# Splitting POOL's rounding of the next tile's inputs over two steps of a fused attention kernel

## The chip, the cores and the metric

One Trainium2 chip, one of its cores. The time is the device time of one execution of the program in microseconds (us); lower is better. PE is TensorE's matrix unit, DVE is VectorE, ACT is ScalarE, POOL is GpSimd, SP is the engine that issues most DMAs.

## The reference

The program is one block of a network on 1024 tokens (16 sequences of 64) of width 256: a gated cross-attention layer and a gated mixture of experts. Cut to what bears on the change:

```python
def _div_clamp_fp8(x, scale):
    y = jnp.clip(x.astype(jnp.float32) / scale, -FP8_MAX, FP8_MAX)
    y = y.astype(jnp.bfloat16).astype(jnp.float32)
    return _fp8_roundtrip(y)              # to float8_e4m3 and back

ln_out = _ln(hidden_states, ln_w, ln_b)
q  = _ln(_fp8_linear_pertensor(ln_out, wq,  ..., q_in_scale),  qln_w, qln_b)    # 16 heads of 128
k  = _ln(_fp8_linear_pertensor(ln_out, wk,  ..., k_in_scale),  kln_w, kln_b)    # 8 heads
v  = _fp8_linear_pertensor(ln_out, wv, ..., v_in_scale)
core = _gqa(q, k, v)                      # softmax attention, two q heads to a k head
qx = _ln(_fp8_linear_pertensor(ln_out, wqx, ..., qx_in_scale), qxln_w, qxln_b)
kx, vx = split(cond @ w_kv_x)             # from the context, kx normalised too
xout = _gqa(qx, kx, vx)
catq = _div_clamp_fp8(concatenate([core, xout]), proj_smooth)
x = x + tanh(g_xattn) * (catq @ wproj * scales)
x = x + tanh(g_ffn) * mixture_of_experts(layernorm(x))
```

Four times per token (for k, q, v and qx) the layer's input is divided by a vector of scales, clamped and rounded to the float8 grid before its projection.

## The kernel before

**Tiles and steps.** The tokens are 8 tiles of 128. Each tile takes four steps, c = 0 to 3, so the attention is 32 steps, numbered n = 4 t + c. `run_steps` (L95 on) writes the first and the last tile out and runs tiles 1 to 6 as a loop of the hardware. A step projects four banks of 512 columns (`BANKS`: k, q, q, v in steps 0 and 1, kx, qx, qx, vx in steps 2 and 3), turns the normalised heads of the step before (`head_transposes`), takes the scores of step n-2, the values of step n-3 and the output projection of step n-4. Each engine has its own hand-written order of the same steps, and semaphores alone tie them. After the attention come the router, the scatter of rows to expert slots, 22 expert units and the gather.

**TensorE in a step** (`step` under `block.tensor`): `project(t, c, 0)` (L868 for kx and vx, L876 for the others), `prob_transposes` (L911), `scores` (L903), `project` 1, `values` (L925), `output` (L935), `project` 2, `head_transposes` 0 (L894), `project` 3, `head_transposes` 1 and 2. `project` of k, q, v and qx waits on `xgrid_done`, t + 1: the rounded inputs of its tile lie in `xq`, a part of the buffer `arena`.

**ACT in a step**: it copies each projected bank out of PSUM (`evacuate`, L645; `values_out`, L653), copies the transposed probabilities (L690), scales bank 0 of the step before by its norm coefficients (`norm_bank0`, L666), takes the softmax's exponential (L685), copies the heads (`heads_out`, L680), and last takes the root of the step's variances (`roots`, L657 and L659), for which it waits for POOL's `va`.

**DVE in a step**: statistics of bank 0 (L1275), `softmax_in` (L1283, L1286), statistics of bank 1, `softmax_sum` (L1292, L1295, which gives `rinv`), statistics of bank 2 (its last one gives `bn_done`), `over_smooth` (L1302) and `quantise`, the five operations of `to_grid` on 1024 columns of 16-bit numbers (L1235, L1237, L1240, L1242, L1246). In step 1 it also does `inputs_magnitude` (L1251, L1253, L1256) for the next tile; in step 3 `residual` (L1316, L1319).

**POOL in a step**: `normalise` (L529, waits for `rinv`), `variance` (L503 and L505, waits for `bn_done`), `coefficients` (L511, L512, L513, L517: four short operations in a chain, of which the first waits for ACT's root), `norm_bank` 1 and 2 (L523). The inputs of tile t + 1 are made on the side, over the steps of tile t: the division in step 0 (`inputs_over_scale`, L472), the clamp and the magnitude by DVE in step 1, and the rounding at the end of step 2 (`inputs_round`, two operations: the addition of a big number, L495, and its subtraction, L497, which gives `xgrid_done`). Tile 0's inputs are made by DVE in the prologue, so POOL rounds seven times, for tiles 1 to 7. POOL's step lags TensorE's: while POOL is at the end of step 2, TensorE is in the later part of step 3.

Of the kernel before, what the change touches and what calls it, by code (L numbers as in the profile page):

```python
# [83 lines left out]
def ge(eng, sem, value):  # L84

    if isinstance(value, int) and value <= 0:
        return
    eng.wait_ge(sem, value)


def live(n, back):

    return not isinstance(n, int) or 0 <= n - back < 4 * NT
# [21 lines left out]
def build(nc, x, cols, rowc, ident, cen, tri, slot, ctxT, wkvN, wqN, wkN, wvN, wqxN, wpT, rwT, wffn, out):  # L115
    ctx = ExitStack()
    with ctx:
# [9 lines left out]
        NU = 4  # L127
# [331 lines left out]
        def _(gp):  # L459
# [4 lines left out]
            def load_output_weights():  # L464

                gp.wait_ge(ld_wkv, 16)
                gp.dma_start(wp[:, :, :], wpT.rearrange("(h p) o -> p h o", p=P)).then_inc(ld_wp, 16)

            def inputs_over_scale(T):
                gp.wait_ge(xT_evac, 4)  # L470
                ge(gp, xgrid_done, T)
                gp.tensor_tensor(xin[:, :].rearrange("p (j c t) -> p j c t", j=4, c=HC),  # L472
                                 xT[:, :, bass.ds(T * P, P)].unsqueeze(1).to_broadcast([P, 4, HC, P]),
                                 sinv[:, :].rearrange("p (j c) -> p j c", j=4).unsqueeze(3)
                                 .to_broadcast([P, 4, HC, P]), ALU.mult).then_inc(xin_done, 1)
# [9 lines left out]
            def chained(sem, ins, count):  # L485

                ins.then_inc(sem, 1)
                gp.wait_ge(sem, count)

            xin16 = xin[:, :].bitcast(F16)  # L490

            def inputs_round(T):

                gp.wait_ge(xmag_done, T + 1)
                gp.tensor_tensor(xin16, xin[:, :], xm[:, :], ALU.add).then_inc(xbig_done, 1)  # L495
                gp.wait_ge(xbig_done, T + 1)
                gp.tensor_tensor(xq[:, bass.ds(T * XW, XW)], xin16, xm[:, :], ALU.subtract).then_inc(xgrid_done, 1)  # L497

            def variance(n, x):

                gp.wait_ge(bn_done, n + 1)
                ge(gp, coef_done, n)
                gp.tensor_tensor(va[:, :], st[:, :, 2], epsc[:, x, :], ALU.add).then_inc(var_done, 1)  # L503
                gp.wait_ge(var_done, n + 1)
                gp.tensor_tensor(vw[:, :], va[:, :], newt[:, 0, :], ALU.mult).then_inc(achain, 1)  # L505

            def coefficients(n):

                gp.wait_ge(achain, n + 1)
                gp.wait_ge(root_done, n + 1)  # L510
                chained(nchain, gp.tensor_tensor(nw[:, 0, :], vw[:, :], r0[:, :], ALU.mult), 3 * n + 1)  # L511
                chained(nchain, gp.tensor_tensor(nw[:, 1, :], nw[:, 0, :], r0[:, :], ALU.mult), 3 * n + 2)  # L512
                chained(nchain, gp.tensor_tensor(nw[:, 0, :], nw[:, 1, :], newt[:, 1, :], ALU.add), 3 * n + 3)  # L513
                ge(gp, norm0_done, n)
                ge(gp, norm1_done, n)
                ge(gp, norm2_done, n)
                gp.tensor_tensor(cw[:, :], nw[:, 0, :], r0[:, :], ALU.mult).then_inc(coef_done, 1)  # L517

            def norm_bank(n, c, i):

                r = raw[c % 2][i].rearrange("p (h d) -> p h d", d=D)
                gp.wait_ge(coef_done, n + 1)
                gp.tensor_tensor(r, r, cw[:, 4 * i:4 * i + 4].unsqueeze(2).to_broadcast([P, 4, D]), ALU.mult)\  # L523
                  .then_inc((norm0_done, norm1_done, norm2_done)[i], 1)

            def normalise(w, s):
                gp.wait_ge(rinv_done, w + 1)
                ge(gp, probT_done, w - 1)
                gp.tensor_tensor(probn[s].rearrange("p (g t) -> p g t", t=S),  # L529
                                 prob[s].rearrange("p (g t) -> p g t", t=S),  # L530
                                 rinv[:, s, :].unsqueeze(2).to_broadcast([P, 8, S]),
                                 ALU.mult).then_inc(probn_done, 1)

            def step(t, c):
                n = NU * t + c
                proj, attend = live(n, 0), live(n, 2)
                if attend:
                    normalise(n - 2, c % 2)
                if proj:
                    variance(n, c // 2)  # L540
                    coefficients(n)
                    norm_bank(n, c, 1)
                    norm_bank(n, c, 2)
                if c == 0 and live(n, -NU):
                    inputs_over_scale(t + 1)
                if c == 2 and live(n, -NU):
                    inputs_round(t + 1)
                if isinstance(n, int) and n == 0:
                    load_output_weights()

# [15 lines left out]

            last = NU * NT
            run_steps(gp, step)
            normalise(last - 2, 0)
            twin_rows(0)  # L570
# [1036 lines left out]
```

## Time and profile before

| | us |
|---|---|
| median of 3 runs | 470.15 (469.44 to 470.99) |
| the profiled execution's own time | 468.51 |
| its span on the core | 466.7 |
| a tile of the loop (four steps) | 39.1 |
| busy share of PE, DVE, ACT, POOL over the span | 89, 80, 63, 60% |

A line of the trace gives the start in us, the duration, the engine, the line of the program, the operation, its output <- its inputs, partitions x elements, and how many operations of that kind stand in a row. In brackets behind it stands how long the engine had stood idle before it, and what ended that. Ends of matmuls are modelled: a line of PE can overlap the next one.

### The profile page before, as it was taken

The page shows a single profiled execution, that of the slowest core. Times are in us where ns is not written, and L with a number is a line of the kernel's source. Part 1 is how long each engine was busy: PE and PEld are TensorE (multiplying, and loading weights), DVE is VectorE, ACT ScalarE, POOL GpSimd, SP SyncE. Part 2 cuts the span into 40 slices and gives each one's busy share as a digit, 9 for nine tenths or more (in the row PEclk, how much of TensorE's full clock was granted, in tenths as well). Part 3 has the DMA queues.
Part 4 walks back from the last instruction along what each step waited for, and adds up shares of the span by engine and source line. Part 5 has one row for each costly group of instructions (what it writes and reads, how often), then busy time and mean ns, then how long its engine had stood idle before and what let it go on. Part 6 is the DMA issues. An engine that isn't in the chain of part 4 may idle for free.

```text
span 466.7 us, 10266 instructions
## 1 busy us (share of the span) xinstructions
PE 413.2 (89%) x3127; PEld 315.6 (68%) x3127; DVE 372.2 (80%) x837; ACT 295.5 (63%) x622; POOL 278.8 (60%) x401
## 2 busy tenths in 40 slices
PE   0488899999999999999999999999989496999980
PEld 0346667767776776777677677677679385999960
DVE  5887889999898999999989889999986763333247
ACT  3578967677776776767777677676882223566620
POOL 2055396686767759667676874965551571377650
PEclk9979999999999999999999999999997789999995
DMA  8944909999920000000000000000086122344308
GB/s 209 270 175 53 129 1 305 253 295 267 269 70 0 0 0 0 0 0 0 0 0 0 0 0 0 0 1 1 2 353 256 56 92 90 109 132 139 103 14 267
DMA packets 34812, 45.68 MB, mean 98 GB/s; under 512 B 3034, under 2 KB 32223, under 8 KB 33888
## 3 DMA queue, kind: packets, MB, share of 16 engines
q1 hardware_dynamic: 26656, 35.61, 25.7%
q0 software_dynamic: 6992, 9.46, 9.3%
q10 hardware_dynamic: 1136, 0.27, 0.3%
q8 instruction: 14, 0.23, 0.2%
q14 instruction: 14, 0.11, 0.1%
HBM read 28.34 MB, written 24.32 MB: 113 GB/s over the span
## 4 chain that ended last, share of the span: by engine, by line
PE 45%; DVE 17%; POOL 15%; issue 10%; ACT 7%; DMA 3%; ACTq 1%; POOLq 1%; SPq 0%; DVEq 0%
PE proj_ps L876 9%; PE score_ps L903 7%; PE pv_ps L925 4%; PE proj_ps L1036 4%; PE headT_ps L1036 4%; PE out_ps L935 4%; POOL xin L495 3%; POOL zbuf L564 3%; POOL rot L523 3%; DVE st L1275 3%; ACT rot L645 2%; PE headT_ps L894 2%; PE probT_ps L911 2%; POOL reg L529 2%; DVE yv L1302 2%
## 5 line engine op out<-in xcount | busy, mean ns | idle before, releaser
L876 PE MATMUL proj_ps<-arena 128*128 128x512 f16 x384 | 100.4, 385 | 3.9 <-POOL arena L497 3.9
L1275 DVE BATCH_NORM_STATS2 st<-rot 128x6 f32<-128x256 f32 x192 | 72.8, 421 | 14.2 <-ACT rot L645 13.2
L645 ACT ACTIVATE rot<-proj_ps 128x512 f32<-128x512 f32 x96 | 56.4, 587 | 20.7 <-PE proj_ps L876 19.1
L523 POOL TENSOR_TENSOR rot<-rot,cw 128x512 f32<-128x512 f32 x64 | 67.3, 1072 | 2.5
L529 POOL TENSOR_TENSOR reg<-reg,rinv 128x512 f32<-128x512 f32 x32 | 34.6, 1082 | 55.2 <-DVE rinv L1295 55.2
L903 PE MATMUL score_ps<-kT,qT 128*128 128x64 f32 x512 | 62.0, 275 | 0.6 <-ACT qT L680 0.5
L903 PEld LDWEIGHTS score_ps<-kT,qT 128*128 128x128 f32 x512 | 60.1, 193 | 2.4 <-ACT qT L680 2.2
L666 ACT ACTIVATE rot<-rot,cw 128x128 f32<-128x128 f32 x128 | 40.9, 390 | 30.3 <-POOL cw L517 30.3
L876 PEld LDWEIGHTS proj_ps<-arena 128*128 (+1 forms) x384 | 37.5, 103 | 29.8 <-issue 6.6
L868 PE MATMUL proj_ps<-arena 128*128 128x512 f16 x192 | 46.7, 379 | 0.0
L587 POOL DMA_INDIRECT ybuf<-arena,bslot x32 | 31.4, 983 | 19.1 <-issue 13.4
L925 PEld LDWEIGHTS pv_ps<-reg,vv 64*128 64x128 f32 x512 | 31.9, 192 | 14.5 <-issue 14.0
L1302 DVE TENSOR_TENSOR yv<-pv_ps,smi 128x512 bf16<-128x512 f32 x64 | 40.7, 677 | 0.0
L925 PE MATMUL pv_ps<-reg,vv 64*128 64x128 f32 x512 | 38.1, 290 | 1.9 <-DVE yv L1302 1.9
L935 PE MATMUL out_ps<-wp_sb,reg 128*128 128x256 bf16 x256 | 36.0, 287 | 4.2 <-DVE reg L1246 4.2
L894 PE MATMUL headT_ps<-idf,rot 128*128 128x128 f32 x256 | 38.5, 273 | 1.2 <-ACT kT L680 1.2
L511 POOL TENSOR_TENSOR nw<-vw,r 128x12 f32<-128x12 f32 x32 | 10.2, 320 | 42.5 <-ACT r L659 42.5
L894 PEld LDWEIGHTS headT_ps<-idf,rot 128*128 128x128 f32 x256 | 30.4, 141 | 7.4 <-issue 1.8
L685 ACT ACTIVATE reg<-reg 128x512 f32<-128x512 f32 x32 | 20.1, 628 | 23.9 <-DVE reg L1286 23.9
L935 PEld LDWEIGHTS out_ps<-wp_sb,reg 128*128 128x128 bf16 x256 | 23.5, 102 | 11.6 <-DVE reg L1246 4.9
L868 PEld LDWEIGHTS proj_ps<-arena 128*128 (+1 forms) x192 | 18.8, 98 | 15.5
L680 ACT ACTIVATE qT<-headT_ps,colv 128x512 f32<-128x512 f32 x32 | 24.9, 779 | 0.1
(220 smaller groups left out, 871.0 us busy)
## 6 DMA issues: line engine op xcount, KB each, us to landing
zbuf<-fill SPq DMA_DIRECT2D x1, 16576.5 KB, 64.4
arena<-in_wffn SPq DMA_DIRECT2D x4, 1536.0 KB, 13.6
arena<-zbuf SPq DMA_DIRECT2D x32, 128.5 KB, 2.1
wkv_stage<-in_wkvN SPq DMA_DIRECT2D x1, 2048.0 KB, 15.2
wp_sb<-in_wpT POOLq DMA_DIRECT2D x1, 2048.0 KB, 15.6
wp_sb<-ybuf SPq DMA_DIRECT2D x8, 256.0 KB, 4.6
xs<-in_x SPq DMA_DIRECT2D x2, 512.0 KB, 5.4
vv<-in_wqN POOLq DMA_DIRECT2D x1, 1024.0 KB, 12.6
```

Source lines behind the costliest of these rows:

```text
L523: gp.tensor_tensor(r, r, cw[:, 4 * i:4 * i + 4].unsqueeze(2).to_broadcast([P, 4, D]), ALU.mult)\
L529: gp.tensor_tensor(probn[s].rearrange("p (g t) -> p g t", t=S), prob[s].rearrange("p (g t) -> p g t", t=S), rinv[:, s, :].unsqueeze(2).to_ ...
L645: act.activation(raw[c % 2][i], proj_ps[i % 2][:, :], ACT.Copy).then_inc(proj_evac, 1)
L666: ins = act.activation(r, r, ACT.Copy, scale=cw[:, h:h + 1])
L868: mm = pe.matmul(ps, lhs, w[:, ch, o:o + 512], start=(k == 0), stop=(k == 5))
L876: mm = pe.matmul(ps, lhs, w[kind][:, ch, 512 * b:512 * b + 512], start=(k == 0), stop=(k == 3))
L894: mm = pe.transpose(dst, raw[c % 2][i][:, h * D:(h + 1) * D], idf[:, :])
L903: mm = pe.matmul(score_ps[:, (2 * g + b) * S:(2 * g + b + 1) * S], qT[:, s, 2 * g + b, :], kT[:, s, g, b * S:(b + 1) * S], start=True, sto ...
L925: mm = pe.matmul(pv_ps[b][:, g * P:(g + 1) * P], vv[rows, u, g * D:(g + 1) * D], pT[rows, g * P:(g + 1) * P], start=True, stop=True)
L935: mm = pe.matmul(out_ps[:, 0:H], catq[u % 2][:, h * P:(h + 1) * P], wp[:, 8 * u + h, :], start=(u == 0 and h == 0), stop=(u == NU - 1 and ...
L1275: ins = ve.bn_stats(st[:, 4 * i + h:4 * i + h + 2, :].rearrange("p h s -> p (h s)"), raw[c % 2][i][:, h * D:(h + 2) * D].rearrange("p (h d ...
L1302: ins = ve.tensor_tensor(y3[:, :, b * S:(b + 1) * S], pv_ps[b][:, :].rearrange("p (h t) -> p h t", t=S), smi[:, 8 * u:8 * u + 8].unsqueeze ...
```

## The change

`inputs_round` becomes two functions, and they are called at other places of POOL's order. The addition now stands in step 2 between `variance` and `coefficients`, the subtraction in step 3 between `variance` and `coefficients`. In both places ACT is about to take the root for which `coefficients` waits. Nothing is added or left out, no other engine's order is touched, and the semaphores are the same.

```diff
-            def inputs_round(T):
+            def inputs_big(T):
 
                 gp.wait_ge(xmag_done, T + 1)
                 gp.tensor_tensor(xin16, xin[:, :], xm[:, :], ALU.add).then_inc(xbig_done, 1)
+
+            def inputs_grid(T):
+
                 gp.wait_ge(xbig_done, T + 1)
                 gp.tensor_tensor(xq[:, bass.ds(T * XW, XW)], xin16, xm[:, :], ALU.subtract).then_inc(xgrid_done, 1)
...
                 if proj:
                     variance(n, c // 2)
+                if c == 2 and live(n, -NU):
+                    inputs_big(t + 1)
+                if c == 3 and live(n, -NU):
+                    inputs_grid(t + 1)
+                if proj:
                     coefficients(n)
                     norm_bank(n, c, 1)
                     norm_bank(n, c, 2)
                 if c == 0 and live(n, -NU):
                     inputs_over_scale(t + 1)
-                if c == 2 and live(n, -NU):
-                    inputs_round(t + 1)
```

POOL in the loop, from its `variance` of step 2 to its `coefficients` of step 3, before. REGISTER_ALU and ISA rows are address and semaphore work.

```order
L503 TENSOR_TENSOR va<-st,epsc 128x12
L505 TENSOR_TENSOR vw<-va,newt 128x12
L511 TENSOR_TENSOR nw<-vw,r 128x12
...
L517 TENSOR_TENSOR cw<-nw,r 128x12
L523 TENSOR_TENSOR rot<-rot,cw 128x512 x2
L494 REGISTER_ALU
L495 TENSOR_TENSOR xin<-xin,xm 128x1024
L497 ISA
L497 TENSOR_TENSOR arena<-xin,xm 128x1024
L529 TENSOR_TENSOR reg<-reg,rinv 128x512
...
L505 TENSOR_TENSOR vw<-va,newt 128x12
L511 TENSOR_TENSOR nw<-vw,r 128x12
```

The addition follows the two norm banks of step 2, and the subtraction follows the addition, ahead of step 3's `normalise`. Now the same stretch (the subtraction has become L500, L503 has become L506, and so on):

```order
L506 TENSOR_TENSOR va<-st,epsc 128x12
L508 TENSOR_TENSOR vw<-va,newt 128x12
L494 REGISTER_ALU
L495 TENSOR_TENSOR xin<-xin,xm 128x1024
L514 TENSOR_TENSOR nw<-vw,r 128x12
...
L526 TENSOR_TENSOR rot<-rot,cw 128x512 x2
L532 TENSOR_TENSOR reg<-reg,rinv 128x512
...
L508 TENSOR_TENSOR vw<-va,newt 128x12
L500 ISA
L500 TENSOR_TENSOR arena<-xin,xm 128x1024
L514 TENSOR_TENSOR nw<-vw,r 128x12
```

The addition has moved up past the four coefficient operations and the two norm banks. The subtraction has moved down past step 3's `normalise` and `variance`, so it now stands behind POOL's waits for `rinv` and for `bn_done` of step 3.

## Rows read from the trace of the kernel before

**Rows 1.** The page: busy time of each engine and its share of the span.

```profile
PE 413.2 (89%) x3127; PEld 315.6 (68%) x3127; DVE 372.2 (80%) x837; ACT 295.5 (63%) x622; POOL 278.8 (60%) x401
```

**Rows 2.** Busy time in one tile: stretch, length, each engine's busy us (operations), TensorE's granted clock.

```profile
144.01:183.14 39.13, 38.40 (x296) 27.97 (x297) 36.23 (x74) 27.80 (x61) 27.94 (x40) 1.00 0.00 0
```

**Rows 3.** The timeline of PE where one tile passes to the next.

```profile
178.95 1.03 PE L876 MATMUL proj_ps<-arena 128*128 128x512 f16 x4
...
180.25 1.46 PE L868 MATMUL proj_ps<-arena 128*128 128x512 f16 x6
...
181.98 0.60 PE L894 MATMUL headT_ps<-idf,rot 128*128 128x128 f32 x4
...
183.14 1.03 PE L876 MATMUL proj_ps<-arena 128*128 128x512 f16 x4 [0.56 <-POOL arena L497]
...
184.31 0.65 PE L911 MATMUL probT_ps<-idf,reg 128*128 128x128 f32 x4
```

**Rows 4.** The timeline of POOL from step 2's variance to step 3's normalise.

```profile
173.10 0.21 POOL L505 TENSOR_TENSOR vw<-va,newt 128x12 f32<-128x12 f32 x1
174.30 0.27 POOL L511 TENSOR_TENSOR nw<-vw,r 128x12 f32<-128x12 f32 x1 [0.99 <-ACT r L659]
...
175.84 0.65 POOL L517 TENSOR_TENSOR cw<-nw,r 128x12 f32<-128x12 f32 x1
...
178.56 2.13 POOL L495 TENSOR_TENSOR xin<-xin,xm 128x1024 f16<-128x1024 bf16 x1
180.88 2.12 POOL L497 TENSOR_TENSOR arena<-xin,xm 128x1024 f16 x1 [0.19 <-POOL xin L495]
182.96 1.22 POOL L529 TENSOR_TENSOR reg<-reg,rinv 128x512 f32<-128x512 f32 x1
```

**Rows 5.** The timeline of DVE in the same stretch.

```profile
173.61 0.43 DVE L1235 TENSOR_SCALAR yv<-yv 128x1024 bf16<-128x1024 bf16 x1
...
175.72 0.69 DVE L1246 TENSOR_TENSOR reg<-ys,ym 128x1024 bf16<-128x1024 f16 x1
...
179.82 0.20 DVE L1295 RECIPROCAL rinv<-sm 128x8 f32<-128x8 f32 x1
180.64 0.77 DVE L1275 BATCH_NORM_STATS2 st<-rot 128x6 f32<-128x256 f32 x2 [0.62 <-ACT rot L645]
...
182.63 0.65 DVE L1235 TENSOR_SCALAR yv<-yv 128x1024 bf16<-128x1024 bf16 x1
...
183.32 1.15 DVE L1237 TENSOR_SCALAR ya<-yv 128x1024 uint16<-128x1024 uint16 x1
```

**Rows 6.** The timeline of ACT in the same stretch.

```profile
176.52 1.28 ACT L666 ACTIVATE rot<-rot,cw 128x128 f32<-128x128 f32 x4 [1.34 <-POOL cw L517]
177.70 0.57 ACT L645 ACTIVATE rot<-proj_ps 128x512 f32<-128x512 f32 x1
178.44 0.63 ACT L685 ACTIVATE reg<-reg 128x512 f32<-128x512 f32 x1 [0.16 <-DVE reg L1286]
180.01 0.60 ACT L645 ACTIVATE rot<-proj_ps 128x512 f32<-128x512 f32 x1 [0.94 <-PE proj_ps L876]
```

**Rows 7.** The timeline of POOL, DVE and PE in tile 0, at the same places.

```profile
54.70 0.21 POOL L505 TENSOR_TENSOR vw<-va,newt 128x12 f32<-128x12 f32 x1
...
58.19 0.21 POOL L511 TENSOR_TENSOR nw<-vw,r 128x12 f32<-128x12 f32 x1 [3.27 <-ACT r L659]
...
63.35 0.76 DVE L1275 BATCH_NORM_STATS2 st<-rot 128x6 f32<-128x256 f32 x2 [0.47 <-ACT rot L645]
...
66.98 0.65 PE L911 MATMUL probT_ps<-idf,reg 128*128 128x128 f32 x4
```

**Rows 8.** The timeline of PE between attention and experts, behind a pause.

```profile
393.67 0.63 PE L1076 MATMUL out_ps<-idf,arena 128*128 128x128 f32 x4 [2.85 <-DMA arena<-zbuf]
```

**Rows 9.** Busy time by stretch (columns as in rows 2), where the clock was low after a pause.

```profile
22.00:30.00 8.00, 6.78 (x36) 3.82 (x36) 7.11 (x13) 4.70 (x9) 5.95 (x2) 0.57 0.84 305
393.00:399.00 6.00, 5.33 (x28) 4.56 (x29) 0.00 (x0) 2.35 (x4) 0.91 (x6) 0.72 0.41 112
```

## The prediction

> **What bounds the kernel now.** I read the busy shares first: PE leads with 89% of the span, DVE follows with 80% [rows 1]. Over a whole tile of the loop PE is busy 38.40 of 39.13 us, at a granted clock of 1.00 [rows 2]. So PE bounds the attention, and it has 0.7 us of slack in a tile. Where is that? The timeline of PE shows it at one place, the passage to the next tile [rows 3]: the first projection of the new tile starts at 183.14 after 0.56 us of waiting for POOL's subtraction, and the transposes of the probabilities behind it start at 184.31, although the projection frees PE at about 184.0 (its neighbour at 178.95 is followed after 0.87 us). They wait for POOL's `normalise`, which ends at 184.18 [rows 4]. Everything else in the loop is dense. Two questions decide the change: when does the subtraction end after it, and does anything else reach PE?
>
> **The change, step 2: the addition moves up.** POOL is done with the variance at 173.31 and waits for ACT's root until 174.30 [rows 4]. The addition takes 2.13 us [rows 4], so it would run from 173.38 to 175.51: 0.9 us are hidden, and 1.2 us push the coefficients back.
>
> There is a second price. At 173.61 DVE begins `quantise` [rows 5], in the middle of the addition. What happens to such a DVE operation while POOL works on SBUF is in the rows of the next step: L1235 takes 0.43 us as a rule, but 0.65 at 182.63, and ends 0.28 us behind the end of POOL's subtraction at 183.00; L1237 takes 1.15 us at 183.32 and ends 0.29 us behind the end of POOL's `normalise` at 184.18 [rows 4, 5]. So it stands still until POOL's instruction is through. Here that means an end at 175.79 instead of 174.04, and **DVE is 1.75 us late**. The addition is first here by 0.2 us. The Trainium skill ("SBUF — State Buffer", section "Who interferes with whom") says the same of these two engines: whichever starts first holds the shared port pair for its whole instruction. By that rule the first sum below is 14 us; without it, some 7 us.
>
> POOL's four coefficient operations then run beside the rest of `quantise`. Beside it they take 0.65 us each, otherwise 0.21 to 0.27 [rows 4]. They end about when L1242 does, 177.5 instead of 176.49. ACT's `norm_bank0` starts at 177.53 instead of 176.52 [rows 6], and ends at 178.8. The transposes of PE that need it come at 179.8, behind the projection of 178.95 [rows 3]: covered, with 1.0 us to spare. ACT's copy of bank 1 ends at 179.4, and the projection of 180.25 needs it: covered by 0.9 us.
>
> DVE ends `quantise` at 178.16 instead of 176.41 [rows 5]. The softmax's difference, which releases ACT's exponential at 178.44 [rows 6], comes at about 180.2. ACT takes 0.63 us for it, and DVE's sum and reciprocal end 0.95 us later as before (179.07 to 180.02), at 181.8. ACT copies bank 2 only behind the exponential, 180.8 to 181.4 instead of 180.01 to 180.61 [rows 6]. DVE's last statistics end at about 182.45 instead of 181.41 [rows 5]. The copy of the heads is 0.8 us late as well, and may cost PE's transposes of 181.98 some 0.2 us.
>
> **Step 3: the subtraction moves down.** It now stands behind `normalise` (waits for `rinv`, 181.8) and the variance (waits for the statistics, 182.45). `normalise` takes 1.04 us when nothing is in its way, the two variance operations 0.5: 183.4. The subtraction adds 2.12 us [rows 4]: **it ends at 185.5 instead of 183.00**. With the same 0.14 us of passage PE restarts at 185.65, having been ready at 182.75: a pause of 2.9 us instead of 0.56. `normalise` is now early, so the transposes follow at once, at 186.5 instead of 184.31 [rows 3]. **PE is 2.2 us later per tile.** The lateness of DVE behind this point (L1235 stands still again, under the subtraction, about 1.9 us) lies within PE's own, and ACT's root, at the end of ACT's step, is ready before POOL asks. As the following steps are dense on PE, nothing gives it back.
>
> Tile 0 is another case [rows 7]. There the root comes only at 58.19, so the addition (54.98 to 57.1) is hidden whole. The last statistics end at 64.11; 0.6 and 2.13 us later the subtraction ends at 66.85, PE restarts at 67.0, and the transposes come at 67.85 instead of 66.98: 0.9 us. Tile 7 has no rounding. First sum: 6 x 2.2 + 0.9 = 14.1 us.
>
> **The clock.** A pause of 2.9 us in each tile is new. The only pause of that length that is followed by steady work is 2.85 us, before the transposes at 393.67 [rows 8], and in the stretch around it the mean granted clock is 0.72 over 6.0 us [rows 9]. With two levels, 1.2 and 2.4 GHz, that is 3.4 us at the lower one, with PE busy throughout: 1.7 us lost. In the prologue the mean is 0.57 over 8.0 us [rows 9], 6.9 us at the lower level, of which PE was busy for some 6: up to 3 us lost. The loop's present waits of 0.56 us leave it at 1.00 [rows 2]. So a fall costs 1.7 to 3 us; I take 2.0, as the nearer row in length and in what follows is the first. I take it for five of the six tiles of 2.9 us, one being spared: 10 us. The Trainium skill ("TensorE: Matmul & The Clock Gate", section "HAM oscillation — how this bites in real kernels") warns of this pattern, waits between bursts of matmuls that throttle the engine again each time. Without that rule the sum stops at 14 us.
>
> **Sum**: 14.1 + 10 = 24 us on the profiled execution's 468.5: 492.6. The median of the runs is 1.6 us above it, so I forecast 494.
>
> **The rivals.**
>
> *The clock holds.* All of the delay, none of the fall: 470.15 + 14.1 = 484. For it: one pause of this length in one place is thin evidence, and around that place PE's work is of another kind (float32 with small tiles) than the loop's dense float16. Against it: both stretches of rows 9. Chance 0.18.
>
> *DVE isn't held.* The addition starts behind DVE's L1235, or the two don't block each other in this form. Then DVE stays on time, the last statistics end at 181.41 as now, and the variance at 182.1; the subtraction ends at 184.35, PE restarts at 184.5 and the transposes come at 185.35: 1.05 us per tile, pauses of 1.8 us and the clock left alone. 6 x 1.05 + 0.9 = 7 us: 477. Against it: 182.63 and 183.32 in rows 5. Chance 0.1.
>
> *PE is caught twice.* `quantise` of step 2 gives the output projection of step 3 its input. At 178.2 it is just when PE wants it. With a little more delay there, PE's third projection, the copy of bank 2, the statistics and the subtraction all shift with it, by 1 us per tile, and a fall costs 3 us in all six: 6 x 3.2 + 0.9 + 18 = 38 us: 508. Chance 0.09.
>
> *The other side: POOL's relief reaches PE.* The 4.3 us of rounding no longer stand between the norm banks and `normalise`, which can start at 180.1 instead of 182.96, and the subtraction is there before PE asks. Then both of PE's waits vanish, 0.56 + 0.3 us in seven tiles: 464. The point from which it decides: the subtraction must end by 182.4, hence start by 180.3, and the variance by 179.7. But DVE's last statistics start at 180.64 even now, after waiting for ACT's copy of a bank that PE projects at 178.95 [rows 3, 5]. Only if the subtraction did not depend on them could it be. Chance 0.03. That the new waits and the gain cancel to within 0.3%, about what a measurement of this kernel can tell from no change: 0.02.
>
> **How the numbers follow.** The forecast's own case has 0.58: with 1.7 to 3 us for a fall, in three to six tiles, it spans 470.15 + 14 + 5 to 14 + 18, or 489 to 502. The range must hold the case of the steady clock too, with some error of its delay: 481 to 503. It leaves out "not held" and the other side (0.15) and most of "twice". Faster 0.03, same 0.02, slower 0.95.
>
> **What would show it.** PE's wait for the subtraction at the first projection of a tile: about 2.9 us, six times, and 1.7 in tile 0 (right); under 1 us would refute step 3. DVE's L1235 at about 2.2 us twice in every tile: the port. POOL's wait for ACT's root gone in steps 2 and 3, DVE's last statistics in step 3 about 1 us later against PE. A tile of 41.3 us with the clock at 1.00, or 43 with a mean below 0.97. A tile of 40.2 us is "not held"; one of 39.1 or less makes all of this wrong.

## The result and the profile after

The changed kernel takes 487.3 us (median of 4 runs, 482.4 to 492.6) against 470.0 for the kernel before. The ratio is 1.033, with an interval of 1.028 to 1.037: slower, on the side and within the range of the forecast, 7 us below its point of 494. Ratios here leave out runs more than 1.5% above the quickest of their kernel (here 492.6 us), while medians keep them. The profiled execution took 488.9 us, with a span of 487.1.

The four runs scatter over 10 us, where those of the kernel before lie within 1.6 us. That alone says little: on another occasion nine runs of the kernel before lay between 475.6 and 484.1 us.

| | before | after |
|---|---|---|
| span of the profiled execution, us | 466.7 | 487.1 |
| PE's first projection of tile 1 starts at | 65.81 | 66.18 |
| a tile of the loop | 39.11 | 41.10 |
| the tile from 272.06, with the clock low for a while | | 44.35 |
| PE's first projection of tile 7 starts at | 300.48 | 316.41 |
| from there to the end | 166.2 | 170.7 |

Busy time of each engine over the whole execution, after [rows 1]:

```profile
PE 417.1 (86%) x3127; PEld 319.7 (66%) x3127; DVE 388.6 (80%) x837; ACT 293.2 (60%) x622; POOL 280.4 (58%) x401
```

The same number of instructions, and 16 us more on DVE alone. By tile, after [rows 2]: stretch, length, busy us of PE, its weight loads, DVE, ACT, POOL, then the granted clock.

```profile
66.18:107.66 41.48, 38.42 (x296) 28.02 (x297) 39.69 (x75) 27.34 (x60) 28.39 (x40) 1.00 0.97 248
189.86:230.96 41.10, 38.25 (x297) 28.01 (x297) 38.45 (x74) 27.45 (x60) 28.26 (x40) 1.00 0.00 0
272.06:316.41 44.35, 41.50 (x296) 30.54 (x297) 38.55 (x74) 27.33 (x60) 28.27 (x40) 0.92 0.00 0
```

PE's work in a tile is what it was (38.3 us), in 2.0 us more. DVE is busy 2.2 us longer without one instruction more. In the last row PE itself is 3.2 us longer busy, at a mean clock of 0.92.

Who waited for whom, after (total us, times, longest):

```profile
POOL reg L532 <- DVE rinv L1301: 77.8, 26, 10.1
POOL nw L514 <- ACT r L665: 34.6, 19, 4.1
PE proj_ps L882 <- POOL arena L500: 18.6, 7, 2.8
```

POOL's waits for ACT's root have shrunk from 42.5 us (32 times) to 34.6 (19 times): that much of the change does what it says. In return POOL waits 22.6 us more for DVE's `rinv`, and PE waits 18.6 us for the subtraction, where it waited 3.9.

The timeline after, where one tile passes to the next, POOL and DVE from step 2's variance on, and PE's restart [rows 3 to 5]:

```profile
177.66 2.13 POOL L495 TENSOR_TENSOR xin<-xin,xm 128x1024 f16<-128x1024 bf16 x1
178.00 2.07 DVE L1241 TENSOR_SCALAR yv<-yv 128x1024 bf16<-128x1024 bf16 x1
...
181.14 0.65 POOL L520 TENSOR_TENSOR cw<-nw,r 128x12 f32<-128x12 f32 x1
...
183.75 0.69 DVE L1292 TENSOR_TENSOR reg<-score_ps,mx 128x512 f32<-128x512 f32 x1
...
184.68 1.46 PE L874 MATMUL proj_ps<-arena 128*128 128x512 f16 x6
...
185.97 0.75 DVE L1281 BATCH_NORM_STATS2 st<-rot 128x6 f32<-128x256 f32 x2
...
186.14 1.04 POOL L532 TENSOR_TENSOR reg<-reg,rinv 128x512 f32<-128x512 f32 x1 [1.80 <-DVE rinv L1301]
...
187.60 2.12 POOL L500 TENSOR_TENSOR arena<-xin,xm 128x1024 f16 x1
187.94 2.06 DVE L1241 TENSOR_SCALAR yv<-yv 128x1024 bf16<-128x1024 bf16 x1
...
189.86 1.03 PE L882 MATMUL proj_ps<-arena 128*128 128x512 f16 x4 [2.83 <-POOL arena L500]
...
190.73 0.60 PE L917 MATMUL probT_ps<-idf,reg 128*128 128x128 f32 x4
```

To lay this beside the trace of before, PE's projection of 180.25 there [rows 3] is the one of 184.68 here: 4.43 us to be taken off. L1241 (the old L1235) stands still under each of POOL's two long operations and ends 0.28 us behind the first (180.07 against 179.79). The last coefficient ends at 177.36 on the scale of before (forecast 177.5), the last statistics at 182.29 (forecast 182.45), the subtraction at 185.29 (forecast 185.5), and PE restarts at 185.43 (forecast 185.65). Behind the restart the transposes follow at once.

### The profile page after: what moved, and what is told of

Its sections match the earlier page's. It is cut to its first block, busy times and chain, and to the rows that moved or that the text cites. A ratio compares the mean times of both kernels' runs of the same rounds, so it can differ in the third digit from the quotient of the medians.

```text
span 487.1 us, 10266 instructions
## 1 busy us (share of the span) xinstructions
PE 417.1 (86%) x3127; PEld 319.7 (66%) x3127; DVE 388.6 (80%) x837; ACT 293.2 (60%) x622; POOL 280.4 (58%) x401
## 4 chain that ended last, share of the span: by engine, by line
PE 46%; POOL 15%; issue 15%; DVE 14%; ACT 6%; DMA 1%; ACTq 1%; another core or an unknown queue 1%; POOLq 1%; SPq 0%; DVEq 0%
PE proj_ps L882 12%; PE score_ps L909 8%; POOL rot L526 6%; PE pv_ps L931 4%; PE out_ps L941 4%; PE proj_ps L1042 4%; PE headT_ps L1042 3%; POOL arena L500 3%; PE headT_ps L900 2%; ACT qT L686 2%; DVE xs L1549 1%; PE probT_ps L917 1%; PE score_ps L1057 1%; POOL nw L516 1%; POOL nw L515 1%
## 5 line engine op out<-in xcount | busy, mean ns | idle before, releaser
L882 PE MATMUL proj_ps<-arena 128*128 128x512 f16 x384 | 101.7, 388 | 18.6 <-POOL arena L500 18.6
L532 POOL TENSOR_TENSOR reg<-reg,rinv 128x512 f32<-128x512 f32 x32 | 33.4, 1043 | 77.8 <-DVE rinv L1301 77.8
L526 POOL TENSOR_TENSOR rot<-rot,cw 128x512 f32<-128x512 f32 x64 | 73.0, 1159 | 2.5
L909 PE MATMUL score_ps<-kT,qT 128*128 128x64 f32 x512 | 65.2, 284 | 0.6 <-ACT qT L686 0.5
L909 PEld LDWEIGHTS score_ps<-kT,qT 128*128 128x128 f32 x512 | 63.3, 201 | 2.4 <-ACT qT L686 2.4
L931 PEld LDWEIGHTS pv_ps<-reg,vv 64*128 64x128 f32 x512 | 33.5, 200 | 15.3 <-issue 14.8
L931 PE MATMUL pv_ps<-reg,vv 64*128 64x128 f32 x512 | 39.7, 298 | 1.9 <-DVE yv L1308 1.9
L1241 DVE TENSOR_SCALAR yv<-yv 128x1024 bf16<-128x1024 bf16 x32 | 36.0, 1125 | 1.1
L514 POOL TENSOR_TENSOR nw<-vw,r 128x12 f32<-128x12 f32 x32 | 9.8, 306 | 34.7 <-ACT r L665 34.6
L874 PEld LDWEIGHTS proj_ps<-arena 128*128 (+1 forms) x192 | 18.8, 98 | 15.5
```

The lines of the kernel that those rows point to most:

```text
L874: mm = pe.matmul(ps, lhs, w[:, ch, o:o + 512], start=(k == 0), stop=(k == 5))
L882: mm = pe.matmul(ps, lhs, w[kind][:, ch, 512 * b:512 * b + 512], start=(k == 0), stop=(k == 3))
L909: mm = pe.matmul(score_ps[:, (2 * g + b) * S:(2 * g + b + 1) * S], qT[:, s, 2 * g + b, :], kT[:, s, g, b * S:(b + 1) * S], start=True, sto ...
L931: mm = pe.matmul(pv_ps[b][:, g * P:(g + 1) * P], vv[rows, u, g * D:(g + 1) * D], pT[rows, g * P:(g + 1) * P], start=True, stop=True)
L1241: ve.tensor_scalar(y, y, FP8_MAX, -FP8_MAX, ALU.min, ALU.max).then_inc(clip, 1)
```

## The experiments

Tiles are compared in their profiled executions: in the loop, with the clock at 1.00, the tiles of one kernel agree within 0.05 us, except the first tile of the loop, which in the kernels with the late subtraction is some 0.4 us longer. What follows the loop differs by several us from kernel to kernel, though none of the edits touches it. The line numbers are those of each kernel and shift by a few.

### Which of the two moves costs what

Only the subtraction moved:

```diff
                 if proj:
                     variance(n, c // 2)
-                if c == 2 and live(n, -NU):
-                    inputs_big(t + 1)
                 if c == 3 and live(n, -NU):
                     inputs_grid(t + 1)
...
+                if c == 2 and live(n, -NU):
+                    inputs_big(t + 1)
```

> Only the subtraction is moved (step 3, behind the variance); the addition stands at the end of step 2 as in the kernel before. Theory (the subtraction's place behind the variance is what PE feels, the addition's place adds 0.8 us of it through DVE's standstill): DVE's last statistics of step 3 are on time, the subtraction ends 1.5 us later than before, a pause of about 2.0 us at the passage, a tile of 40.3 us, 478 us in all. Rival (the addition's place does most of the harm): a tile near 39.1 us, 470 us. Rival (the addition's place is harmless): a tile of 41.1 us, 483 to 487 us.

Measured: 477.2 us, ratio 1.014 (1.011 to 1.018), a pause of 1.79 us.

```profile
226.85:266.85 40.00, 38.18 (x296) 28.05 (x296) 36.73 (x74) 27.65 (x60) 27.97 (x41) 1.00 0.00 0
```

The tile is 0.9 us longer than before, not 2.0. The subtraction's place costs 0.9 us, and 1.1 us are the addition's. Theory held; its 40.3 us were 0.3 too many.

Only the addition moved:

```diff
+                if c == 2 and live(n, -NU):
+                    inputs_big(t + 1)
                 if proj:
                     coefficients(n)
...
                 if c == 2 and live(n, -NU):
-                    inputs_round(t + 1)
+                    inputs_grid(t + 1)
```

> Only the addition is moved (step 2, behind the variance); the subtraction stands at the end of step 2, ahead of step 3's normalise, as before. Theory (PE feels only the subtraction's end and normalise): the subtraction ends some 0.5 us before PE asks, DVE's L1235 in step 2 still stands still for 1.6 us and is covered, both waits of PE at the passage vanish, a tile of 38.3 to 38.6 us, 465 to 467 us, faster than the kernel before. Rival (the held DVE and the late coefficients reach PE by themselves): a tile over 39.5 us, 473 us or more.

```profile
221.14:259.64 38.50, 38.43 (x299) 28.03 (x298) 36.72 (x74) 27.39 (x61) 28.16 (x41) 1.00 0.00 0
```

The tile is 38.5 us, 0.6 **shorter** than before, and PE waits for POOL at no passage. L1242 still takes 2.07 us in step 2: the standstill alone hurts nobody as long as the subtraction doesn't stand behind DVE's statistics. The whole time stays unclear: 465.6, 468.7, 475.5 and 475.6 us in four runs, around the 469.8 of the kernel before. The gain in the loop is shown, that in the total isn't. The 10 us of scatter come here without one long wait of PE in the loop.

### The standstill or the late coefficients

The addition of the changed kernel does two things in step 2: it holds DVE's L1235, and it makes the four coefficient operations late. First it was moved to where it does neither, behind the coefficients:

```diff
-                if c == 2 and live(n, -NU):
-                    inputs_big(t + 1)
...
                 if proj:
                     coefficients(n)
+                if c == 2 and live(n, -NU):
+                    inputs_big(t + 1)
+                if proj:
                     norm_bank(n, c, 1)
```

> The changed kernel, but the addition of step 2 stands behind the four coefficient operations and ahead of the two norm banks, where DVE has just finished quantise. Theory (the addition holds DVE by the port, and that makes DVE's last statistics of step 3 1.0 us late): L1235 of step 2 takes 0.43 us again, the statistics are on time, a pause of 2.0 us, a tile of 40.3 us, 478 us. Rival (DVE's standstill is covered, the subtraction's place alone counts): a tile of 41.1 us as in the changed kernel, 483 to 487 us.

```profile
225.95:265.83 39.88, 38.18 (x296) 28.04 (x296) 36.62 (x74) 27.65 (x60) 27.89 (x40) 1.00 0.00 0
```

476.7 us, ratio 1.014 (1.011 to 1.017), and L1242 in step 2 takes 0.43 us. So the addition's 1.1 to 1.2 us per tile go with its place, and come back. This run doesn't say by which of the two ways.

For that the addition was put at the head of step 2, and short operations took its place in the wait for the root:

```diff
+                if c == 2 and live(n, -NU):
+                    inputs_big(t + 1)
                 if attend:
                     normalise(n - 2, c % 2)
                 if proj:
                     variance(n, c // 2)
                 if c == 2 and live(n, -NU):
-                    inputs_big(t + 1)
+                    for k in range(10):
+                        gp.tensor_tensor(spare[:, k, :], epsc[:, 0, :], newt[:, 0, :], ALU.add)
```

Without the short operations, as the base:

> The addition at the head of step 2 (as in the fast order), the subtraction in step 3 behind the variance (as in the changed kernel). Every theory: the subtraction's place alone costs what it cost with the addition at the end of step 2, a tile of 39.9 to 40.0 us, a pause of 1.7 to 1.8 us. It is the base for the next run.

Measured: 39.84 us a tile, pause 1.64 us.

```profile
225.84:265.68 39.84, 38.18 (x296) 28.06 (x296) 36.58 (x74) 27.66 (x60) 27.97 (x40) 1.00 0.00 0
```

With five of them:

> The same, with five additions of 12 columns (constants, into a spare buffer) on POOL in step 2, where the changed kernel has the addition of 1024 columns. They delay the four coefficient operations by about as much (the last ends some 1 to 1.5 us late) but none of them lasts long enough to hold DVE. Theory (DVE's standstill makes the statistics late, not the late coefficients): DVE's L1235 of step 2 stays under 0.7 us, the tile stays at 39.9 to 40.1 us. Rival (the late coefficients, through ACT's norm_bank0 and its copy of bank 1, are what reaches PE): a tile of 40.8 us or more.

Measured: 39.84 us a tile, but this told nothing. The five took 1.06 us together, and the last coefficient ended only 0.1 us later than in the kernel before. (On the chip of these two runs the kernel before took 477.6 us, 475.6 to 484.1, so their whole times, 481.3 and 485.9, are not laid beside those of the other kernels.) With ten:

> As the run before, with ten short additions instead of five, since five took 1.06 us together and moved the end of the coefficients by only 0.1 us. Ten take 2.1 us or more, so the last coefficient should end 1.0 us or more late, as in the changed kernel. Theory (DVE's standstill makes the statistics late, not the late coefficients): L1235 of step 2 stays under 1 us and the tile at 39.8 to 40.1 us. Rival (the late coefficients reach PE): a tile of 40.8 us or more.

```profile
176.38 2.71 POOL L549 TENSOR_TENSOR spare<-epsc,newt 128x12 f32<-128x12 f32 x10
176.71 0.49 DVE L1246 TENSOR_SCALAR yv<-yv 128x1024 bf16<-128x1024 bf16 x1
...
180.25 0.21 POOL L521 TENSOR_TENSOR cw<-nw,r 128x12 f32<-128x12 f32 x1
...
182.28 0.77 DVE L1286 BATCH_NORM_STATS2 st<-rot 128x6 f32<-128x256 f32 x2 [0.48 <-ACT rot L656]
...
183.35 1.46 PE L879 MATMUL proj_ps<-arena 128*128 128x512 f16 x6
```

```profile
269.61:309.81 40.20, 38.18 (x296) 28.01 (x296) 37.09 (x74) 27.53 (x60) 29.86 (x50) 1.00 0.00 0
187.54:229.40 41.86, 39.84 (x296) 29.16 (x296) 37.18 (x74) 27.65 (x60) 29.87 (x50) 0.96 0.00 0
```

Now the coefficients are as late as in the changed kernel (its projection L879 is 3.10 us behind the one of 180.25 before, so 180.46 is 177.36 there, the very number of the changed kernel), and DVE's L1246 is not held: 0.49 us. The ten operations slow the five of `quantise` by 0.05 to 0.06 us each, 0.3 us in all, but that isn't what decides: the second statistics behind them still wait 0.48 us for ACT's copy of bank 1. The tile is 40.20 us, 0.36 above its base. In the changed kernel the tile is 41.10. So of the addition's 1.26 us above this base, **late coefficients by themselves, through ACT, can make 0.36, and the 0.9 us that remain need the standstill**. (In the changed kernel the second statistics don't wait for ACT at all, since DVE is later than the copy; there the standstill may account for the whole 1.26.) My own expectation of 39.8 to 40.1 gave the first way nothing. This kernel was run once: 480.9 us, beside 470.6 for one run of the kernel before.

### The subtraction between normalise and variance

```diff
+                if c == 3 and live(n, -NU):
+                    inputs_grid(t + 1)
                 if proj:
                     variance(n, c // 2)
-                if c == 3 and live(n, -NU):
-                    inputs_grid(t + 1)
```

(the addition stays where the changed kernel has it)

> The changed kernel, but in step 3 the subtraction stands behind normalise and ahead of the variance. Theory (every POOL instruction ahead of the subtraction and its wait counts by its own time): it ends 0.5 to 0.6 us earlier, a pause of 2.3 us, a tile of 40.5 to 40.6 us. The variance and ACT's root come 2.1 us later, but behind PE's restart, where nothing waits for them yet. 479 to 482 us. Rival (the later root holds up PE's first head transposes of the next tile): a tile of 41.1 us or more, 484 us or more.

```profile
187.30:229.50 42.20, 39.81 (x296) 29.00 (x296) 38.07 (x74) 27.68 (x60) 28.20 (x40) 0.96 0.00 0
229.50:270.12 40.62, 38.23 (x296) 28.03 (x296) 37.97 (x74) 27.70 (x60) 28.20 (x40) 1.00 0.00 0
```

481.2 us, a tile of 40.62 and a pause of 2.36 us, 0.47 shorter than with the variance ahead. POOL's two short variance operations count by their own time; the later root costs nothing. As the theory had it.

### The clock

Matmuls whose result the next projection overwrites fill most of the pause:

```diff
                 ps = proj_ps[i % 2][:, :]
                 first = isinstance(t, int) and t == 0
+                if c == 0 and i == 0 and not first:
+                    for _ in range(11):
+                        pe.matmul(ps, xq[:, 0:P], whi["k"][:, 0, 0:512], start=True, stop=True)
```

> The changed kernel, with 11 extra matmuls of 512 float16 columns (about 2.4 us at the full clock) on PE at each passage to the next tile, into the PSUM bank that the next projection overwrites, ahead of its wait for the subtraction. Theory (the pauses cost 2.0 us per tile by themselves, and on top of that let the clock fall in some tiles, which scatters the runs): the pause shrinks to about 0.4 us, the tiles stay at 41.1 us, the granted clock stays at 1.00 from tile 1 to tile 7, the median falls to about 483 us and its runs lie within 2 us of each other. Rival (the scatter and the slow tile have another cause, the clock falls without the pauses too): low stretches in the loop and a spread of 8 us or more as before, median 487.

```profile
231.52:272.63 41.11, 40.65 (x307) 29.02 (x307) 38.45 (x74) 27.46 (x60) 28.26 (x40) 1.00 0.00 0
```

484.0 us (480.4 to 485.3, six runs), PE's wait 0.42 us, and every tile of the loop but the first at 41.1 us, all with a clock of 1.00. The low stretches in the loop are gone. The runs lie within 5 us of each other and not within 2; where the scatter that is left arises, these runs don't show. The medians are 484.0 here and 487.3 there, but the runs overlap, and no fall in six tiles is little against two in six, so the stronger test is the next pair, with a longer pause:

```diff
                 gp.wait_ge(xbig_done, T + 1)
+                gp.tensor_tensor(spare[:, :], xin16[:, 0:XW // 2], xm[:, 0:XW // 2], ALU.subtract)
                 gp.tensor_tensor(xq[:, bass.ds(T * XW, XW)], xin16, xm[:, :], ALU.subtract).then_inc(xgrid_done, 1)
```

> The changed kernel with one more POOL subtraction of 512 columns (about 1.1 us, into a spare buffer) ahead of the subtraction. Theory (PE's restart follows POOL's end one to one, and the longer the pause the more often the clock falls, each time for 3.2 us): a pause of 3.9 us, tiles of 42.2 us with the clock at 1.00 and of 45.4 us with a fall, falls in at least four of the six tiles, 500 us. Rival (falls are not tied to the pauses): 42.2 us in nearly all tiles, at most one or two falls, 492 to 495 us.

> The same longer pause with 16 extra matmuls of 512 float16 columns (3.4 us) on PE ahead of its wait. Theory (the fall needs the idle PE, not the late subtraction): all tiles at 42.2 us and a clock of 1.00 in the loop, 490 us, 10 us below the longer pause left empty. Rival (falls are not tied to the pauses): no difference between the two.

Left empty (first two rows) and filled (the third, from the filled kernel's own trace):

```profile
157.33:201.35 44.02, 39.89 (x296) 29.30 (x296) 39.34 (x74) 27.58 (x60) 29.35 (x42) 0.96 0.00 0
201.35:248.59 47.24, 43.09 (x296) 31.52 (x296) 39.35 (x74) 27.47 (x60) 29.37 (x42) 0.89 0.00 0
```

```profile
194.83:237.23 42.40, 41.74 (x312) 29.51 (x312) 39.28 (x74) 27.51 (x60) 29.39 (x41) 1.00 0.00 0
```

Empty, the kernel takes 509.0 us (507.8 to 511.7), filled 491.8 (489.7 to 492.4), with the same pause in POOL's order and 16 more matmuls per tile. The ratios to the kernel before, 1.086 (1.083 to 1.090) and 1.050 (1.047 to 1.052), don't touch. The 17 us between the two go with PE's idleness, the only thing in which these two kernels differ. Empty, all seven passages are followed by a low stretch, and tiles come in three lengths, 44.0, 45.6 and 47.2 us: the 42.4 of the filled kernel and 1.6, 3.2 or 4.8 more. So a fall costs one, two or three portions of 1.6 us. The low stretches behind them last about 3.4, 6.9 and 10.3 us, at a granted clock of 0.50, which is the lower of the two levels, 1.2 GHz. My expectation had a single price of 3.2 and 500 us.

Put together, the passages of all profiled executions by PE's wait there:

| PE's wait at the passage | passages | with a low clock behind them |
|---|---|---|
| 1.6 to 1.9 us | 30 | 0 |
| 2.0 us (ten short operations) | 6 | 2 |
| 2.4 us (subtraction ahead of the variance) | 6 | 1 |
| 2.8 us (the changed kernel) | 6 | 2 |
| 2.9 us (the longer pause, tile 0) | 1 | 1 |
| 4.1 us (the longer pause, tiles 1 to 6) | 6 | 6 |

Between 2.0 and 2.8 us waits that agree within 0.02 us in one trace go both ways; what decides between them isn't shown.

### The order that gains

```diff
+                if c == 2 and live(n, -NU):
+                    inputs_big(t + 1)
                 if attend:
                     normalise(n - 2, c % 2)
                 if proj:
                     variance(n, c // 2)
                     coefficients(n)
...
                 if c == 2 and live(n, -NU):
-                    inputs_round(t + 1)
+                    inputs_grid(t + 1)
```

> The addition stands at the head of step 2, ahead of normalise, where POOL waits 2.8 us for rinv and DVE runs nothing that a POOL operation holds up; the subtraction at the end of step 2, ahead of step 3's normalise. Theory (both operations are out of every chain that reaches PE): DVE's busy time per tile falls back to some 35.5 us, PE never waits for the subtraction, a tile of 38.3 to 38.5 us like the kernel with the early addition, 465 us, 1% faster than the kernel before. Rival (the subtraction right behind the norm banks still keeps normalise from PE, or DVE becomes the bound): 39.0 us a tile, 469 to 470 us.

```profile
165.39 2.13 POOL L495 TENSOR_TENSOR xin<-xin,xm 128x1024 f16<-128x1024 bf16 x1
168.22 1.04 POOL L532 TENSOR_TENSOR reg<-reg,rinv 128x512 f32<-128x512 f32 x1 [0.70 <-DVE rinv L1302]
...
174.97 2.13 POOL L500 TENSOR_TENSOR arena<-xin,xm 128x1024 f16 x1
177.06 1.05 POOL L532 TENSOR_TENSOR reg<-reg,rinv 128x512 f32<-128x512 f32 x1
...
178.83 1.03 PE L883 MATMUL proj_ps<-arena 128*128 128x512 f16 x4
```

```profile
215.27:253.41 38.14, 38.12 (x298) 28.11 (x297) 35.27 (x74) 27.66 (x61) 27.43 (x40) 1.00 0.00 0
```

462.8 us (460.8 to 470.8, six runs) against 468.8 of the kernel before on the same chip; ratio 0.989 (0.986 to 0.992), a gain of 1.1%, small but clear of the noise. A tile of 38.14 us, PE busy for 38.12 of it. The addition stands in POOL's wait for `rinv`, of which 0.70 us are left; DVE is never held by it and is busy 35.3 us instead of 36.2. The subtraction ends at 177.1, and PE takes up the next tile at 178.83, 1.7 us later, without a wait. The expected time was 465.

## Why the prediction was right, and where a term was off

**The bound and the passage: right.** PE stayed the bound, the loop was dense but for the passage, and with the clock at 1.00 all that a tile loses is PE's wait there: 2.27 us more, less the 0.3 us that the transposes no longer wait. The total of that wait is 18.6 us in seven passages.

**Step 3, the subtraction behind the statistics: right.** It ends 2.3 us later than before (forecast 2.5), the pause is 2.83 us (forecast 2.9). The run that moves the subtraction alone shows that this place costs 0.9 us by itself.

**Step 2, DVE held by the addition: right, a little too large.** L1241 takes 2.07 and 2.06 us in steps 2 and 3, and the chain to the last statistics is as worked out. The term "2.2 us per tile" measured 1.99. The prediction followed the late coefficients to PE and called them covered by 0.9 us. They are covered there, but in the run with ten short operations DVE's second statistics wait for the same copy of ACT's, and through them 0.36 us reach the subtraction. In the changed kernel this is hidden by DVE's larger lateness, so the number didn't suffer; that was luck, as the prediction didn't look at this path.

**Tile 0: right.** The wait there is 1.64 us (forecast 1.7). The transposes come at 67.06 instead of 66.98, which looks like nothing. But PE runs 0.74 us ahead of the trace of before from 30 us on, long before the first of the moved operations. With that taken off, the change puts tile 0's transposes off by 0.82 us (forecast 0.9). The next tile, 41.48 us instead of 39.11, carries 0.4 us more than the others, which the prediction didn't have; where they arise wasn't looked into. Together 0.82, 2.37 and five times 1.99: 13.1 us; forecast 14.1.

**The clock: the mechanism right, its frequency and its price off.** The term that missed is "I take it for five of the six tiles of 2.9 us, one being spared: 10 us". In the profiled execution two of the six long waits are followed by a low stretch, at 272 and at 316, and each costs 3.2 us (44.35 less 41.10 for the first), where I had put 2.0. That makes 6.4 us instead of 10, too many falls at too low a price: the two errors partly cancel, and that is luck. The trace of before had one pause of this length only, and I made a rule of it. It also held more on the price than the one stretch that I used. These are its three low stretches in the part behind the loop:

```profile
353.50:360.50 7.00, 7.00 (x42) 6.31 (x42) 5.25 (x30) 1.91 (x2) 0.10 (x1) 0.51 0.49 208
367.00:377.50 10.50, 6.27 (x30) 4.44 (x27) 8.26 (x19) 0.75 (x3) 8.28 (x8) 0.51 0.27 97
394.50:398.00 3.50, 3.50 (x15) 2.73 (x14) 0.00 (x0) 2.18 (x4) 0.47 (x4) 0.51 0.41 114
```

They last about 6.9, 10.3 and 3.4 us, the same three lengths as in the loop, and I priced a fall by the shortest. The first of them shows one thing more: PE had no wait longer than 0.8 us in the ten us ahead of it (it ran float32 and small tiles there). So a long wait isn't the only thing behind which the clock falls.

That some runs have more falls than others could be a part of the scatter of 482 to 493 us. Only one of the four was profiled, so this is argued, not shown, and it is hardly all of it: the kernels with the early addition scatter by 10 us too (465.6 to 475.6, 460.8 to 470.8), and their profiled executions have no low stretch in the loop.

**What is left.** 13.1 + 6.4 - 0.74 (the prologue) = 18.8 us; the span grew by 20.4. The other 1.6 us are lost behind the attention. DVE's first operation on the last tile's router output stands waiting there, with a releaser that the profile can't name, in a place where the kernel before had none:

```profile
DVE arena L1407 <- remote: 2.8, 1, 2.8
```

Whether this belongs to the change or to the execution wasn't tried. In the 13 traces the part from the last subtraction to the end takes 165.9 to 174.8 us, with the falls in tile 7 taken off, and the kernels are the same there. So I take it for the latter; that is not shown. The median adds to the miss: I put it 1.6 us above the profiled execution, as for the kernel before, and it lies 1.6 below. Of the 6.7 us between 494 and 487.3, 3.2 are this and not the kernel.

**The rivals.** "The clock holds" (484 us) is what the filled kernel gives, 484.0. The changed kernel's own clock did not hold. "DVE isn't held" asked for tiles 1.05 us longer; the runs with the late subtraction in which DVE isn't held in step 2 have 0.73 to 0.89 us, and 1.09 with the late coefficients on top, whose 0.36 us the rival didn't have. "PE is caught twice" didn't come: PE's output projection kept its place. "The other side" named its own condition, a subtraction that doesn't depend on the statistics, and both orders that keep to it are faster per tile than the kernel before, 38.50 and 38.14 us.

## What to carry to other kernels

An engine's idle time is worth filling only where the work that is put in has all its inputs, holds nobody, and isn't wanted before the wait behind which it now stands is over. The wait for ACT's root failed two of the three: in step 2 the addition fell on DVE's 16-bit operations, and in step 3 the subtraction came to stand behind two waits that it had had no need of. For the addition, the wait for `rinv`, a few instructions earlier on the same engine, met them all.

On a kernel that TensorE bounds, a pause of TensorE is to be priced twice: once by its length, and once by the clock. The second was 6.4 us beside 13.1 here, and some 17 us in the kernel with the longest pauses. Waits of the same length were followed by a fall or not, so one profile gives a price for its own execution and not for the median. The scatter of the runs doesn't tell it either, since kernels without such waits scatter as much; filling the wait and measuring again does.

## What the runs showed of the hardware

- A DVE tensor-scalar operation on 16-bit numbers in SBUF that starts under a long POOL operation on SBUF ends 0.28 or 0.29 us behind POOL's end: 2.07 us instead of 0.43 here. A chain of ten POOL operations of 12 columns held the same operation for 0.06 us. The Trainium skill ("SBUF — State Buffer", "Who interferes with whom") has the lock for the whole instruction, and every such row here agrees. Not every DVE operation is held: `over_smooth`, which reads one input from PSUM, ran its usual 1.27 us for two under the subtraction in the trace of before:

```profile
102.66 2.12 POOL L497 TENSOR_TENSOR arena<-xin,xm 128x1024 f16 x1 [0.19 <-POOL xin L495]
103.11 1.27 DVE L1302 TENSOR_TENSOR yv<-pv_ps,smi 128x512 bf16<-128x512 f32 x2
```

- POOL's short operations beside DVE's 16-bit ones take up to 0.65 us, and 0.21 without them (L517 before, 0.65; L521 with ten short operations, 0.21); DVE's own durations hardly change beside a single one (0.43 us).
- A clock that falls after a pause costs this loop 1.6 us or two or three times that, in tiles that otherwise agree within 0.05 us. At the passages of the loop it was never seen behind 30 waits of 1.6 to 1.9 us, it came behind 5 of 18 of 2.0 to 2.8 us, behind the one of 2.9 us and behind all six of 4.1 us. Keeping PE at work on results that nobody reads took 17 us off the kernel with the longest pauses.
